# A convolution tap moved from VectorE to TensorE, a reset moved from a DMA to GpSimd, and GpSimd's pacing waits taken out

## The reference

```python
q = _causal_dwconv(x @ Wq.T, cq_w, cq_b)      # depthwise, 4 taps, along time
k = _causal_dwconv(x @ Wk.T, ck_w, ck_b)
v = _causal_dwconv(x @ Wv.T, cv_w, cv_b)
g = jax.nn.log_sigmoid(x @ Wg.T); beta = jax.nn.sigmoid(x @ Wb.T)
k = k / jnp.clip(jnp.linalg.norm(k, axis=-1, keepdims=True), 1e-12, None)
q = q * Kd ** (-0.5)
def step(S, inp):                             # one token after the other
    Sk = jnp.einsum('bhkv,bhk->bhv', S, k_t)
    delta = jnp.einsum('bhv,bhk->bhkv', v_t, k_t) - jnp.einsum('bhv,bhk->bhkv', Sk, k_t)
    S = jnp.exp(g_t)[..., None, None] * S + b_t[..., None, None] * delta
    return (S, jnp.einsum('bhkv,bhk->bhv', S, q_t))
o = o.reshape(b, t, H * Kd) @ Wo.T
```

## Time and profile before

| | |
|---|---|
| median of three runs | 1710.75 us |
| the profiled execution's own time | 1710.73 us |
| its span, first to last instruction | 1708.9 us |
| what lies around the span | 1.8 us |
| mean granted TensorE clock | 0.967 of 2.4 GHz |
| PE / DVE / ACT / POOL busy over the span | 1516.3 / 1241.4 / 882.6 / 763.7 us |
| PE / DVE busy from 160 to 1060 us | 854.62 / 853.03 of 900 us |

### The profile page before, as it was taken

How to read it: one execution, slowest core, us unless ns; L and a number is a source line. 1 busy time by engine, 2 the same in 40 slices (tenths; PEclk the granted TensorE clock), 3 DMA queues, 4 the chain that set the end, 5 groups by cost and what they waited for, 6 DMA issues and landing times. The chain is left out here.

```text
span 1708.9 us, 70110 instructions
## 1 busy us (share of the span) xinstructions
PE 1516.3 (89%) x29196; PEld 1129.7 (66%) x29196; DVE 1241.4 (73%) x3125; ACT 882.6 (52%) x2282; POOL 763.7 (45%) x1038
## 2 busy tenths in 40 slices
PE   6679999999999999999999999677999998899980
PEld 6235666666666666666666666566899998887870
DVE  1498999999999999999999999533566665222225
ACT  1476776777777777777777677320111111333333
POOL 0133333333333333333333333312777777677775
PEclk9989999999999999999999999888999999999995
DMA  8345555556656656655655655526565631799658
GB/s 322 94 88 121 123 123 128 138 121 130 140 117 133 140 114 134 135 120 128 142 124 125 133 124 122 119 59 210 161 189 164 188 98 42 213 255 252 131 86 304
DMA packets 525995, 247.30 MB, mean 145 GB/s; under 512 B 424400, under 2 KB 490576, under 8 KB 524784
## 3 DMA queue, kind: packets, MB, share of 16 engines
q1 hardware_dynamic: 372432, 202.55, 44.5%
q10 hardware_dynamic: 134784, 21.25, 7.4%
q0 software_dynamic: 18464, 19.03, 6.2%
HBM read 171.39 MB, written 71.37 MB: 142 GB/s over the span
## 5 line engine op out<-in xcount | busy, mean ns | idle before, releaser
L391 PE MATMUL delta_p_j<-xt,w 128*128 128x512 f32 x768 | 387.7, 628 | 20.3 <-PEq L56 7.7
L584 DVE SCALAR_TENSOR_TENSOR delta_kq<-delta_hist,cw,delta_kq 128x512 f32<-128x512 f32 x384 | 288.4, 751 | 21.1 <-ACT delta_kq L737 13.1
L904 POOL TENSOR_TENSOR delta_sd<-state,eg_end 128x256 f32<-128x256 f32 x128 | 79.4, 620 | 392.4 <-DVE delta_yv L597 205.7
L730 ACT ACTIVATE delta_hist<-delta_p_j 128x512 f32<-128x512 f32 x192 | 114.7, 597 | 230.0 <-PE delta_p_j L391 228.9
L391 PEld LDWEIGHTS delta_p_j<-xt,w 128*128 128x128 f32 x768 | 131.8, 191 | 136.0 <-issue 101.9
L1408 POOL DMA_INDIRECT slot_tokens<-tokens,mix_slot x192 | 189.2, 985 | 64.3 <-issue 53.7
L898 POOL TENSOR_TENSOR delta_root<-delta_n,half_power 128x8 f32<-128x8 f32 x64 | 106.5, 1664 | 246.8 <-DVE delta_kq L584 246.8
L640 DVE TENSOR_TENSOR delta_xi<-delta_xi,delta_outer 128x15 f32<-128x15 f32 (+7 forms) x480 | 143.8, 300 | 16.5
L597 DVE SCALAR_TENSOR_TENSOR delta_yv<-delta_hist,cw,delta_yv 128x512 f32<-128x512 f32 x192 | 143.7, 748 | 4.7 <-ACT delta_yv L737 2.4
L446 PEld LDWEIGHTS delta_p_i<-delta_kkq,rt 64*32 64x32 f32 (+1 forms) x4096 | 67.2, 100 | 108.4 <-DVE delta_kkq L647 100.2
L1178 PE MATMUL mix_p_h<-wo,w 128*88 128x128 f32 x1024 | 126.2, 277 | 13.3 <-ACT wo L1364 13.0
(11 more groups left out here) (152 smaller groups left out, 3261.3 us busy)
## 6 DMA issues: line engine op xcount, KB each, us to landing
delta_xd<-x_scratch SPq DMA_DIRECT2D x256, 128.0 KB
w<-in_wqkv SPq DMA_DIRECT2D x64, 384.0 KB, 3.6
w<-in_w SPq DMA_DIRECT2D x64, 352.0 KB
delta_eg<-eg_rows SPq DMA_DIRECT2D x128, 130.0 KB
n_scratch<-delta_kkq ACTq DMA_DIRECT2D x128, 128.0 KB
ot<-o SPq DMA_DIRECT2D x128, 128.0 KB, 3.0
w<-in_w SPq DMA_DIRECT2D x64, 176.0 KB
xt<-ot SPq DMA_DIRECT2D x8, 1024.0 KB
```

What stands on the lines that cost most here:

```text
L391: mm = pe.matmul(p_j[:, :], w[e][:, (ch * 3 + n) * 128:(ch * 3 + n) * 128 + 128], xt[m // 8 % 2][:, ch * 512:ch * 512 + 512], start=ch == ...
L584: ve.scalar_tensor_tensor(out, view(hist[e], i * 2 * 518 + tap, (259, 2), (1, 256)), cw[:, column:column + 1], out, ALU.mult, ALU.add).the ...
L730: ac.activation(view(hist[e], n * 518 + 3, (259, 2), (1, 256)), p_j[:, :], ACT.Copy)
```

## The change

The first tap (tap 0) of the value convolution leaves DVE. `turn_values` on PE, which transposes by `yv^T I`, adds `hist^T diag(w0)` into the same PSUM tile; the diagonal matrices come with the projection weights, whose tile grows from 768 to 832 columns. On GpSimd the three pacing waits go, `roots` serves macro t-1 behind `weight` with a single buffer, and a copy of 256 columns resets `xi` in place of the DMA. ACT scales a macro's values a part earlier. DVE's calls stand in another order.

```diff
-WCOLS = 2 * 3 * 128
+WCOLS = 2 * 3 * 128 + C
...
-        sq, n2, root, rn, bp, fk = sb("sq", 512), sb("n2", 8), two("root", 8), sb("rn", 8), sb("bp", 8), sb("fk", 8)
+        sq, n2, root, rn, bp, fk = sb("sq", 512), sb("n2", 8), sb("root", 8), sb("rn", 8), sb("bp", 8), sb("fk", 8)
...
                 sp.wait_ge(kk_out[group % 2], 64 * (group // 2 + 1))
-                if group >= 1:
-                    sp.wait_ge(x_out[(group - 1) % 2], 16 * ((group - 1) // 2 + 1))
-                    sp.wait_ge(xit_out, group)
-                sp.dma_start(xi[:, :], a["const"][:, C_EYE:C_EYE + SUB * SUB]).then_inc(xi_set, 16)
                 sp.dma_start(view(kb, 0, (SUB, SUB), (1, SUB)),
...
             def turn_values(m, chunks):
-                pe.wait_ge(conv_v, 3 * m + 3)
+                pe.wait_ge(conv_v, 2 * m + 2)
                 for c in chunks:
-                    for b, h in QUADS:
-                        mm = pe.matmul(view(p_xy, b * 512 + 256 + c * C, (1, C), parts=half(h ^ b)),
-                                       view(yv[e], b * 256 + c * C, (1, C), parts=half(h)),
-                                       view(const, C_ID + 64 * h, (1, C), parts=half(h)), start=True, stop=True)
+                    for first in (True, False):
+                        for b, h in QUADS:
+                            if first:
+                                token = view(yv[e], b * 256 + c * C, (1, C), parts=half(h))
+                                taps = view(const, C_ID + 64 * h, (1, C), parts=half(h))
+                            else:
+                                token = view(hist[e], 518 + b * 259 + c * C, (1, C), parts=half(h))
+                                taps = view(w[e], 768, (1, C), parts=half(h))
+                            mm = pe.matmul(view(p_xy, b * 512 + 256 + c * C, (1, C), parts=half(h ^ b)), token, taps,
+                                           start=first, stop=not first)
...
                 if is_macro(before):
                     conv_values(before, 1)
-                    conv_values(before, 0)
                     conv(before, 1, tap_q, conv_q)
                     gate(before)
                 if one:
                     update(*one)
                 if even:
-                    substitute(subst_group, range(7, 10))
+                    substitute(subst_group, range(8, 11))
                 if is_macro(m) and t % 2:
                     conv(m, 0, tap_k, conv_k)
                 if two_:
                     residual(*two_)
+                if even:
+                    substitute(subst_group, range(11, SUB - 1))
+                if is_macro(m) and t % 2 == 0:
+                    conv(m, 0, tap_k, conv_k)
+                if odd:
+                    substitute(subst_group, range(0, 2))
                 if is_macro(before):
                     lengths(before)
                 if odd:
-                    substitute(subst_group, range(0, 2))
-                if even:
-                    substitute(subst_group, range(10, 12))
+                    substitute(subst_group, range(2, 4))
                 if is_macro(before):
                     inverse_lengths(before)
-                if odd:
-                    substitute(subst_group, range(2, 4))
-                if even:
-                    substitute(subst_group, range(12, SUB - 1))
-                if is_macro(m) and t % 2 == 0:
-                    conv(m, 0, tap_k, conv_k, (2, 1))
                 if is_macro(mi):
                     horner(mi, rx_done, 16, y1_out)
-                if is_macro(m) and t % 2 == 0:
-                    conv(m, 0, tap_k, conv_k, (0,))
                 if odd:
-                    substitute(subst_group, range(4, 7))
+                    substitute(subst_group, range(4, 8))
                 if two_:
                     update(*two_)
-                if is_macro(m):
+                if is_macro(m) and t % 2 == 0:
                     conv_values(m, 2)
                 if is_macro(mi):
                     horner(mi, ry1_done, 32, y2_out)
+                if is_macro(m) and t % 2:
+                    conv_values(m, 2)
                 if is_macro(before):
                     mask(before)
...
-                if is_macro(t - 3):
-                    scale_values(t - 3, range(4, 8))
+                if is_macro(t - 2):
+                    scale_values(t - 2, range(0, 4))
...
                 if is_macro(t - 2):
-                    scale_values(t - 2, range(0, 4))
+                    scale_values(t - 2, range(4, 8))
...
             def roots(m):
-                po.wait_ge(clipped, m + 1)
-                if m >= 2:
-                    po.wait_ge(vp_out, 8 * (m - 1))
-                po.tensor_tensor(root[m % 2][:, :], n2[:, :], view(s.half_power, 0, (0, 8)), ALU.pow).then_inc(small, 1)
+                if m >= 1:
+                    po.wait_ge(vp_out, 8 * m)
+                po.tensor_tensor(root[:, :], n2[:, :], view(s.half_power, 0, (0, 8)), ALU.pow).then_inc(small, 1)
...
-                if is_macro(before):
-                    po.wait_ge(conv_v, 3 * before + 1)
                 if one:
                     decay_state(*one)
...
                     carry_out(before)
-                if is_macro(before):
-                    po.wait_ge(conv_q, 3 * before + 3)
-                if is_macro(t - 2):
-                    roots(t - 2)
+                if t % 2 and 0 <= (t - 3) // 2 < NG:
+                    group = (t - 3) // 2
+                    if group >= 1:
+                        po.wait_ge(x_out[(group - 1) % 2], 16 * ((group - 1) // 2 + 1))
+                        po.wait_ge(xit_out, group)
+                    po.tensor_copy(xi[:, :], const[:, C_EYE:C_EYE + SUB * SUB]).then_inc(xi_set, 1)
                 if two_:
-                    po.wait_ge(r_out, two_[0] * 4 + two_[1] + 1)
                     decay_state(*two_)
                 if is_macro(before):
                     clip(before)
                     factors(before)
                     weight(before)
+                    roots(before)
...
+    diag = np.zeros((NPAIR, 2, C, C), np.float32)
+    diag[:, :, np.arange(C), np.arange(C)] = g["attn_cv_w"][:, 0, 0].reshape(NPAIR, 2, C)
...
-        "wqkv": f(wqkv),
+        "wqkv": f(np.concatenate([wqkv, diag.reshape(NPAIR, 128, C)], 2)),
```

More of the change, by code:

```diff
@@ L572, in _, with conv @@
         def _(ve):
-            def conv(m, i, tapped, done, taps=(2, 1, 0)):
+            def conv(m, i, tapped, done):
                 e = m % 2
                 out = view(kq[e], i * 512, (256, 2), (1, 256))
-                for tap in taps:
+                for tap in (2, 1, 0):
                     if tap == 2:
@@ L594, in conv_values @@
                 else:
-                    ve.wait_ge(conv_v, 3 * m + 2 - tap)
+                    ve.wait_ge(conv_v, 2 * m + 1)
                 column = (m % NPAIR * 3 + 2) * (TAPS + 1) + tap
@@ L633, in substitute @@
                         ve.wait_ge(kb_in, 16 * (group + 1))
-                        ve.wait_ge(xi_set, 16 * (group + 1))
+                        ve.wait_ge(xi_set, group + 1)
                     else:
@@ L792, in scale_values @@
                     at = ring(m) + 512 + g * C
-                    ac.activation(kpv[:, at:at + C], kpv[:, at:at + C], ACT.Copy, scale=root[m % 2][:, g:g + 1]).then_inc(vp_out, 1)
+                    ac.activation(kpv[:, at:at + C], kpv[:, at:at + C], ACT.Copy, scale=root[:, g:g + 1]).then_inc(vp_out, 1)
             def output(group):
```

## The result

The changed kernel takes 1730.7 us, the median of 4 runs (1725.6 to 1736.5), against 1710.9 us of the kernel before in the same session (1710.7 to 1714.0, 4 runs): a ratio of 1.0112, interval 1.0079 to 1.0147. It is slower by 1.1%, on the side that was forecast, inside the range, and 13 us above the predicted 1718. Its profiled execution took 1728.8 us, 18.1 more than the one of before. Lines of the kernel after stand two or so off (L586 the key taps, L599 the value taps, L628 the mask, L902 `sd`, L872 `noff`, L890 `weight`, L896 `roots`).

The account below looks back on a forecast made before the run. DVE was taken to set the pace, PE close behind. Per pair -1.58 (tap) + 0.36 (reciprocal) + 1.55 (collisions) = +0.33 us, times 28 +9, less 2 early: 1718 us; own range 1714 to 1740, whole range 1692 to 1740.

Parts of the forecast that it names:

- the collisions: GpSimd without pacing meets DVE's two-input instructions: new collisions of 1.55 us a pair of slots, bounds 0 and about 3.3.
- the second `sd`: The second chunk's `decay_state`, behind L663, meets key taps in odd and substitution in even slots: 0.3 us each.
- tap 2 in odd slots: In odd slots L904 waits for L663 and meets value tap 2 at the start: 0.15 us a pair.
- the copy: GpSimd's 256-column, one-input copy into `xi`: 0.15 us a pair, bounds 0 and 0.62.
- The wait in front of the reciprocal: In even slots DVE waits for POOL's clip between reduction and reciprocal: +0.36 us a pair, 0 to 0.5.
- The rival of 1811 us: `roots` holds DVE too, 1.66 us a slot, +93 us; chance 0.06 together with collisions at full length.
- While DVE stays slower than this, PE's extra costs nothing: PE's 16 extra matmuls a macro, 0.56 us a slot, were priced at nothing against PE's idle 0.82.
- The figure for 32.8 us a pair: At that pair length PE has 1.4 us slack less 1.1 for its new matmuls, so it doesn't bound.
- the faster rival: DVE's saving goes through, new collisions costing at most half: -0.5 us a pair or less, 1692 us; chance 0.30.
- The work of DVE is unchanged. 0: Substitution, key taps and horner in another order and earlier scaling on ACT: same instructions, priced at 0.
- same: Gain and loss cancel: collisions of 1.1 to 1.3 us a pair, within 3.4 us of 1710.7; chance 0.14.
- a forecast −2: In the six or so slots before the steady stretch, only part of the tap's saving comes through: -2 us.

Follow-up runs that it names:

- e4: The kernel before with only GpSimd's three pacing waits taken out: 1727.1 us, ratio 1.0095 to the kernel before.
- e8: The kernel after with the reduction ahead of the three key taps in even slots: 1717.1 us, ratio 1.0017 to the kernel before.
- e6: The kernel before with PE's 16 extra matmuls a macro, against matrices of zeros, DVE keeping all taps: 1727.8 us, ratio 1.0090.
- e5: The kernel before with tap 0 of the values left out on both DVE and PE: 1688.2 us, ratio 0.9867.
- e1: The kernel before with only tap 0 of the values moved from DVE to PE: 1712.9 us, ratio 1.0015.
- e3: The kernel after with GpSimd's whole stream and ACT's scaling as before; tap 0 on PE and DVE's new order stay: 1727.4 us, ratio 1.0109.
- e9: The kernel before with DVE's calls moved so that `weight` meets instructions that read PSUM: 1792.9 us against 1799.8, ratio 0.9958.
- e2: The kernel after with the wait for the second residual put back before the second `decay_state`: 1735.3 us, ratio 1.0157 to the kernel before.
- e12: e9 with the reciprocal one key tap earlier in even slots: 1779.8 us against 1789.0 of the kernel before, ratio 0.9950.
- e7: The kernel after with `roots` back in mid-slot, its wait, two buffers and ACT's old scaling: 1717.4 us, ratio 1.0033 to the kernel before.

## Why the prediction was right, and where it was off

**The sign held, and the collisions came where they were forecast.** They cost +1.24 us a pair against 1.55: `noff` 0.67 for 0.65, the second `sd` 0.25 and 0.39 for 0.3 each, tap 2 in odd slots 0.24 for 0.15, but the copy nothing for 0.15, and `weight` 0.2 less than before where no difference was forecast. The mask still hides `noff` in odd slots, as forecast. The wait in front of the reciprocal is 0.36 us each time, as forecast. e4 shows collisions by themselves, e8 takes the reciprocal's wait out.

**`roots` does not hold DVE.** In an odd slot of the kernel after it starts at 628.03 and runs 1.66 us beside substitution instructions with two SBUF inputs, each at its usual 0.22:

```profile
628.03 1.66 POOL L896 TENSOR_TENSOR delta_root<-delta_n,half_power 128x8 f32<-128x8 f32 x1
```

```profile
628.43 0.22 DVE L642 TENSOR_TENSOR delta_xi<-delta_xi,delta_outer 128x60 f32<-128x60 f32 x1
628.68 0.22 DVE L639 TENSOR_TENSOR delta_outer<-delta_xi,delta_kb 128x63 f32<-128x63 f32 x1
628.94 0.22 DVE L642 TENSOR_TENSOR delta_xi<-delta_xi,delta_outer 128x63 f32<-128x63 f32 x1
```

The rival of 1811 us is refuted. The Trainium skill, "SBUF — State Buffer", section "SBUF: two separate sides", has the first of GpSimd and a two-input VectorE instruction hold the ports for its whole length: the trace agrees for `weight`, `sd` and `noff`, which wait for the running tap and hold the next (for 0.2 to 0.4 us less than their own time), and not for the power over 8 columns. But `roots` itself was not 1.66 us: behind the tap of an even slot it took 2.11, which puts `noff` 0.45 us later still. The prediction had named over 2 us as a sign against itself; what it missed is that `roots` stretches by waiting, without holding anything.

**The step that failed: "While DVE stays slower than this, PE's extra costs nothing".** Added alone these matmuls cost 0.9% (e6), and the tap without them is worth 1.33% (e5), not the full 0.79 us a slot. Together they are +0.15% (e1). I read PE's 45.4 us of idle time as slack because DVE had almost none; but the runs fit another reading, that DVE had almost none because PE's results came just in time. (The figure for 32.8 us a pair was wrong too: with 30.8 us busy PE has 2.0 us of slack there, not 1.4. Nothing hung on it.) The chance of 0.30 for the faster rival rested on that reading. Its price, 1692 us, is near what e5 gives without PE's part, not what the edit gives; its condition, new collisions under 1.2 us a pair, is met in e1 with none, and e1 is not faster.

**"The work of DVE is unchanged. 0", for the new order** failed as well: e3 against e1 is +16 us, where the forecast had 10 for the reciprocal and nothing else.

**Why the sum still came near: in part by luck.** These costs overlap. The order costs 16 us with the pacing (e3 against e1), the pacing's removal 16 us in the order before (e4), and the whole change 19 us. Where DVE is held by POOL it no longer waits for PE and `kb`: those waits, the reciprocal's among them, were 41 us in e3 and are 16 in the kernel after. A sum over DVE alone could serve because in the kernel after, as in the one before, DVE is again the late one (L649's and L628's waits for PE are 6 us of 900). Its waits in the window from 160 to 1060 us:

```profile
DVE delta_kqg L609 <- DVE delta_kq L586: 10.0, 48, 0.6
DVE delta_rn L620 <- POOL delta_n L877: 9.8, 27, 0.4
DVE delta_kkq L649 <- PE delta_p_i L448: 5.1, 12, 1.0
DVE delta_kqg L609 <- PE delta_p_c L519: 1.0, 5, 0.2
DVE delta_kkq L628 <- PE delta_p_xy L439: 0.9, 2, 0.6
```

They sum to 26.8 us, the three rows of before under e1 to 14.9. From the ninth mask to the last but one, where DVE's instructions and the steps between them can be added up without a remainder, a pair changed by −1.49 us for two taps, +1.24 held, +0.44 waits (0.36 of it the reciprocal's) and +0.33 in the steps from the end of one instruction to the start of the next: +0.52. The last term comes from the order: the reduction and the reciprocal stood between instructions that wait for each other, and overlapped their neighbours (the reciprocal at 615.79 in the earlier trace rows costs 0.11 us from start to start and lasts 0.19). So the forecast had the collisions 0.3 us too dear and put at nothing some 0.4 us that the new order costs. With the measured collisions its own sum gives −1.58 + 0.36 + 1.24 = +0.02 us a pair, 1709 us, "same". That the two errors nearly cancel is luck.

**The 13 us.** 5 us are the loop (13.9 for 9). 5 are the first eight slots, +2.8 for a forecast −2: DVE's waits from 77 to 203 us sum to 12.9 us in the profile after and to 6.9 before (7.1 and 4.1 of it the mask's for PE), so there the tap's time went into waits. 2 stand before the first mask, and they go with the clock and not with the change: from 43 to 86 us the granted clock was 0.84 in the profile after and 0.92 before, and over all the profiles the first mask goes by the clock: at 78.5 to 80.1 us in the nine with 0.84, e4 and e9 among them, which leave PE's work as it was, and at 76.6 to 77.4 us in the five with 0.92, e2 and e8 among them, which have all of the change's. The last 2 are the median against the profiled execution, and 0.7 come back in the last slot and behind it.

The window from 43 to 86 us in the kernel before, and then after (the clock is the third number from the end):

```profile
43.00:86.00 43.00, 26.60 (x207) 11.42 (x205) 21.41 (x31) 18.05 (x38) 5.16 (x13) 0.92 0.33 95
```

```profile
43.00:86.00 43.00, 28.29 (x268) 12.75 (x267) 19.38 (x27) 17.17 (x36) 4.16 (x10) 0.84 0.31 87
```

**What stays open.** How much of PE's extra is its own 0.49 us a slot (forecast 0.56) and how much the later start of what follows in its queue was not separated, nor why `kb` lands late in e3 and hardly so in the kernel after. That PE's results come just in time is read from the waits of e1, e5 and e6; no run moved those results alone.

## What to carry to other kernels

An idle share of a few per cent on the second busiest engine of a coupled loop need not be slack: before pricing work moved onto it at nothing, ask whether its results come just in time. Where two engines hold each other up, it can pay more to place the other engine's instructions under those of the busy one that leave it alone (here the ones that read PSUM; e9 and e12 gained 0.4 to 0.5%) than to move work off the busy one (e1 gained nothing). A wait that uses nothing of what it waits for can be such a placement; take it out only with its collisions priced, and expect the costs of several such edits to overlap.

## What the runs showed of the hardware

- A small GpSimd instruction waits for a running tap too: the copy of 18 columns took 0.66 us (617.49) in place of 0.20, that of 256 columns 0.91 in place of 0.40 (e7: 396 ns mean over 27). In the kernel after that copy held no tap; in e7, where it comes first, the tap beside it took 0.97 us (615.02) for 0.75.
- What a GpSimd instruction of two inputs costs the DVE instruction behind it is its own time less 0.2 to 0.4 us: 0.61 for `weight` of 1.04, 0.75 for `noff` of 1.00 (3.07 less 2.32), 0.39 for `sd` of 0.62 against a substitution row, 0.24 against a tap (three of them from 621.35 to 623.83, 2.48 us for 2.24).
- DVE instructions that read PSUM lose nothing beside any of them: the mask is 1210 to 1225 ns long in the kernel after, in which `noff` runs beside it in half of the slots.
- A power over 8 columns takes 1.66 us and leaves DVE alone, but waits for a running tap like the others (2.11 us).
